# Issuing the fp32r products of K and of the expert layers in pieces of 256 columns instead of 512

## The reference

```
ln_c  : normalise over the 128 channels
q,k,v = w_qkv (768 x 128) applied to the channels; 8 heads of 32
k     = softmax of k over the 1024 pixels
ctx   = k v^T per head; out = ctx^T q;  x = x + w_out out + b_out

t     = x as tokens (16 x 1024 tokens of 128);  tn = ln_t(t)
w     = softmax(mean over images of tn @ Wr + br)      # 8 experts per pixel
for each expert e:
    h = relu(bn1(tn @ W1[e] + b1[e]))
    h = relu(bn2(h  @ W2[e] + b2[e]))
    y += w[:, e] * (h @ Wo[e] + bo[e])
x     = t + y
```

## Time and profile before

| what | us |
|---|---|
| median of 3 runs | 821.94 |
| lowest and highest | 819.64, 822.42 |
| the profiled execution, whole | 819.77 |
| its span, first to last instruction | 818.0 |
| PE busy in the span | 791.9 (97%), 4186 products |
| PEld busy | 669.9 (82%), 4186 loads |
| DVE, ACT, POOL busy | 525.6, 443.5, 578.8 |
| mean granted clock of TensorE | 0.989 of full |

### The profile page before, as it was taken

One profiled execution on the slowest core, in us unless ns is written; L12 is line 12 of the kernel. 1 busy time (PEld: TensorE's weight loads), 2 busy tenths in 40 slices (PEclk: granted clock), 3 DMA queues, 4 the chain that ended last, 5 costly groups with the idle time before them and its releaser, 6 DMA issues.

```text
span 818.0 us, 12728 instructions
## 1 busy us (share of the span) xinstructions
PE 791.9 (97%) x4186; PEld 669.9 (82%) x4186; DVE 525.6 (64%) x999; ACT 443.5 (54%) x560; POOL 578.8 (71%) x497
## 2 busy tenths in 40 slices
PE   6999999999998799999999999999999999999997
PEld 5998999999987678888888888888888888888885
DVE  4688777877865446665665656656656566565663
ACT  2576767767675554554554545545455455454542
POOL 5558788787857168667766776777777776677665
PEclk9999999999999889999999999999999999999999
DMA  7124344343342160210101201102022020110100
GB/s 240 53 79 161 123 163 147 112 170 128 131 154 103 54 231 1 78 65 13 77 26 51 77 0 77 54 23 77 1 77 77 0 77 26 51 77 0 51 26 26
DMA packets 22107, 64.52 MB, mean 79 GB/s; under 512 B 2608, under 2 KB 6840, under 8 KB 22080
## 3 DMA queue, kind: packets, MB, share of 16 engines
q1 hardware_dynamic: 22080, 64.19, 21.4%
HBM read 38.98 MB, written 25.20 MB: 78 GB/s over the span
## 4 chain that ended last, share of the span: by engine, by line
PE 64%; ACT 1%; DVE 0%; POOL 0%; POOLq 0%; issue 0%; DVEq 0%
PE psum L552 63%; PE psum L505 1%; PE psum L621 0%; POOL xn_lo L1045 0%; POOLq L83 0%; ACT h_hi L731 0%; PE psum L608 0%; DVE x_res L985 0%; DVE w_raw L928 0%; ACT xn_hi L743 0%; ACT route_all L767 0%; PE psum L584 0%; ACT feat_most L754 0%; ACT z_early L736 0%; ACT xn2T L695 0%
## 5 line engine op out<-in xcount | busy, mean ns | idle before, releaser
L912 DVE SCALAR_TENSOR_TENSOR h_lo<-psum,h_hi 128x1024 fp32r<-128x1024 f32 x128 | 156.8, 1225 | 207.4 <-ACT h_hi L731 207.4
L731 ACT ACTIVATE h_hi<-psum 128x1024 fp32r<-128x1024 f32 x128 | 131.3, 1026 | 255.9 <-PE psum L552 255.9
L1045 POOL TENSOR_TENSOR h_lo<-w_raw,h_hi 128x1024 fp32r<-128x1024 f32 x64 | 154.1, 2408 | 53.5 <-ACT h_hi L743 53.5
L552 PE MATMUL psum<-h_hi,w_hi 128*128 128x512 f32 x384 | 120.4, 395 | 1.7 <-DVE w_raw L928 0.9
L928 DVE SCALAR_TENSOR_TENSOR w_raw<-psum,minus_t,route_all 128x1024 f32<-128x1024 f32 x94 | 119.9, 1275 | 1.3 <-DMA route_all<-route_scratch 1.3
L552 PE MATMUL psum<-h_hi,w_lo 128*128 128x512 f32 x384 | 120.5, 395 | 0.0
L552 PE MATMUL psum<-h_lo,w_hi 128*128 128x512 f32 x384 | 119.5, 393 | 0.0
L1045 POOL TENSOR_TENSOR xn_lo<-w_raw,xn_hi 128x1024 fp32r<-128x1024 f32 x32 | 78.1, 2441 | 51.9 <-ACT xn_hi L743 51.9
L1045 POOL TENSOR_TENSOR xn_lo<-feat_most,xn_hi 128x1024 fp32r<-128x1024 f32 x32 | 77.2, 2413 | 51.0 <-ACT xn_hi L743 51.0
L1024 POOL TENSOR_TENSOR ln<-ln,const 128x8 f32<-128x8 f32 x32 | 52.6, 1643 | 57.6 <-DVE ln L896 57.6
L552 PEld LDWEIGHTS psum<-h_hi,w_hi 128*128 128x128 f32 x384 | 72.7, 190 | 17.5 <-issue 1.3
(11 more groups left out here) (146 smaller groups left out, 1445.1 us busy)
## 6 DMA issues: line engine op xcount, KB each, us to landing
route_all<-in_x SPq DMA_DIRECT2D x16, 512.0 KB, 3.9
x_res<-in_x SPq DMA_DIRECT2D x16, 512.0 KB, 3.3
x_scratch<-x_res SPq DMA_DIRECT2D x16, 512.0 KB, 2.8
xn_scratch<-xn SPq DMA_DIRECT2D x16, 512.0 KB, 2.6
xs_in<-xn_scratch SPq DMA_DIRECT2D x16, 512.0 KB, 4.5
x_res<-x_scratch SPq DMA_DIRECT2D x16, 512.0 KB, 3.2
out<-x_res SPq DMA_DIRECT2D x15, 512.0 KB, 2.6
route_all<-route_scratch SPq DMA_DIRECT2D x6, 512.0 KB, 6.2
```

The source lines that it names most:

```text
L552: mm = pe.matmul(dst[:, px], w[:, which, e, :], part[:, px], start=first and w is w_hi and part is hi, stop=last and part is lo, skip_grou ...
L731: nc.scalar.activation(h1_hi[r][:], z1[r], ACT.Relu).then_inc(h1_hi_done, 1)
L912: nc.vector.scalar_tensor_tensor(out=h1_lo[r][:], in0=z1[r], scalar=0.0, in1=h1_hi[r][:].bitcast(F32), op0=ALU.max, op1=ALU.subtract).then ...
L1045: nc.gpsimd.tensor_tensor(h2_lo[r][:], h2w[r], h2_hi[r][:].bitcast(F32), ALU.subtract).then_inc(h2_lo_done, 1)
```

## The change: pieces of 256 columns

A constant `PIECE = 256` is added. In `k_half` each product of 512 columns becomes two of 256 columns, one behind the other, with the same weights. In `layer` the loop over two banks becomes a loop over four pieces, again inside the loop over the three part products. The columns, the sums and the order of the part products stay. Only the first piece in a bank carries the start flag.

```
+PIECE = 256
@@ k_half
                     for w, xs in ((wkT_hi, xn_hi), (wkT_lo, xn_hi), (wkT_hi, xn_lo)):
-                        mm = pe.matmul(k_out[j][:, px], w[:, half], xs[p][:, px],
-                                       start=w is wkT_hi and xs is xn_hi, stop=xs is xn_lo)
+                        for m in range(BANK // PIECE):
+                            part = slice(px.start + PIECE * m, px.start + PIECE * (m + 1))
+                            mm = pe.matmul(k_out[j][:, part], w[:, half], xs[p][:, part],
+                                           start=w is wkT_hi and xs is xn_hi and m == 0, stop=xs is xn_lo, skip_group_check=True)
                     mm.then_inc(k_done, 1)
@@ layer
                 for w, part in ((w_hi, hi), (w_lo, hi), (w_hi, lo)):
-                    for n in range(2):
-                        px = slice(BANK * n, BANK * (n + 1))
+                    for n in range(PIXELS // PIECE):
+                        px = slice(PIECE * n, PIECE * (n + 1))
                         mm = pe.matmul(dst[:, px], w[:, which, e, :], part[:, px],
-                                       start=first and w is w_hi and part is hi, stop=last and part is lo, skip_group_check=True)
+                                       start=first and w is w_hi and part is hi and px.start % BANK == 0,
+                                       stop=last and part is lo, skip_group_check=True)
```

## The result

The change costs 12 us. The median of four runs is 832.91 us (832.47 to 833.89) against 820.79 (818.98 to 822.42, four runs), a ratio of 1.0157 with a 95% interval of 1.0135 to 1.0179. The direction and the wide range of the forecast (825, 805 to 864) held. Its size didn't: +3 was forecast, and the forecast's own range, 820 to 830, was missed too.

A forecast was written before the change was run, and what follows sets the result against it. PE was taken to bound the kernel; 2490 pairs at +1.2 ns add 3.0 us to the profiled 819.77, giving 822.8, and the median's 2.2 above the profiled run made it 825. Own range 820 to 830, wide range 805 to 864.

The forecast's parts named there:

- PE bounds both kernels, only the pitch counts: Whole kernel: its time is PE's time, so only two products of 256 columns against one of 512, start to start, matter.
- 2490 products more, each with its own load: K and the layers: 192 plus 2298 products are split, adding 2490 weight loads, from two to four per part product.
- Rival 4: Split products: the chip leaves out a repeated load of the same weights; no chance given.
- The load is hidden beneath 256 columns: Split products: a load occupies 0.111 to 0.114 us and just fits beneath a stream of at least 0.107 us.
- rival 3: Split products: loads don't hide beneath dense fp32r streams, so each piece pays load and stream; +553 us, about 1375, chance 0.05.
- The price of a pair, +1.2 ns: K and the layers: two pieces cost 1.2 ns more than one product of 512, the middle of two ends; +3.0 us.
- 15.7 ns: Products of 512 columns at full clock: the measured pitch of 229.0 ns beyond the 213.3 ns their columns need.
- lower end: Split pairs: the excess is a slower stream, 2.24 columns a ns, and halves with the columns; a pair costs 229.0, change nothing.
- upper end: Split pairs: a rate and a fixed 2.4 ns per product, as fp32 showed; 2490 x 2.4 = 6.0 us.
- Rival 1: Split products: the excess is a fixed start-up per fp32r product, a pair costs 244.7; +39.1 us, 861, chance 0.22.
- Rival 2: Split products: short streams run at full rate and the load limits, a pair costs 223; -15 us, 807, chance 0.20.
- K as 192 pairs of the same price: K's products: their pitch of 0.234 instead of 0.229 changes nothing, as they are only 192 pairs.

## Why the prediction was wrong

- **PE bounds both kernels, only the pitch counts.** Right. Nothing else on the page moved but one pause of 3 us, and the pitch gives 13.6 us, where 12.1 (medians) and 14.1 (profiles) were measured.
- **2490 products more, each with its own load.** Right, 6676 are listed. Rival 4 is out.
- **The load is hidden beneath 256 columns.** Right: 111.2 and 111.4 by itself in the fp32r streams of 128 and 192, as the fp32 rows had given. Load and stream one behind the other would have cost some 550 us (rival 3). The rule of the Trainium skill (TensorE: Matmul & The Clock Gate, "What overlaps and what doesn't"), that a load overlaps products only when its row group differs, is refuted for fp32r at this density by the 117.9 ns of a piece with its load.
- **The price of a pair, +1.2 ns.** This is the step that failed, in two ways. Its lower end, that the 15.7 ns are a slower stream and halve with the columns, is wrong: at a difference of 0 the excess is per product, 13.3 ns at 256 to 512 columns alike, and in the kernel's layers it is 16.5 at 512 and 11.2 at 256, where a rate would leave 8.2. (The 15.7 itself was 0.8 short, being read from window counts.) I had three signs for a rate, and none was one. The excess vanished at half clock, but a fixed excess does so as well. The last pair before a pause took 0.63 us as all others, but the end of a product is modelled in these records, and a duration can't show what a pitch does. And fp32's rows are silent on fp32r; they were also misread, for 0.109 us on 128 columns are two cycles at 2.4 GHz per column, not two half-clocked ones. The upper end, +2.4, took fp32's fixed part for fp32r's. Measured is 5.9 per pair of the layers, 2298 x 5.9 = 13.6 us, where the term had 2490 x 1.2 = 3.0; K, changed alone, cost nothing (819.54 against 819.33). Why a piece costs 117.9 here and not the 113.3 that the same tiles also showed stays open.
- **Rival 1, fixed 15.7 per product, +39 us.** Its mechanism is right at a difference of 0, where the change costs 30.4. It was 27 us off here because the price of a product isn't one number.
- **Rival 2, a piece at 111 to 112, -15 us.** For K's pieces it came near (113.3 in most rounds), and with strips at 192 for all of them, where the change gained 14.0. The reason given (a long stream that runs dry) isn't what was found.
- **K as 192 pairs of the same price.** Wrong, though it moved the time by about 1 us only, and to be seen in the earlier trace rows had I asked: 234 instead of 230 for the same product is a sign that place matters. I called it nothing because it was few pairs.
- **What would show it.** The marks were 873, 855, 817, 897 and 443 products in 100 us. 851 came (848 by the starts), next to "rate and the fixed part in full", which is close to the right number by luck, for a wrong reason; only the streams at several widths separated them.

## What to carry to other kernels

Where a pitch has a part that its columns don't explain, one width can't tell a rate from a fixed part: a stream of the same product at three widths can, in one short run, for the placement it has. If two places in one profile show different pitches for the same instruction, as 230 and 234 here, the reason may be worth more than the change at hand: three strips of 64 bytes gained 7.6 us, and the best width depended on the strips. A pitch may also have more than one stable value at one placement, so look at it before and behind each pause before you credit a change with it. For fp32r, compare placements at the width in use, and widths at a fixed placement, before either is called better.

## What the runs showed of the hardware

- fp32r products back to back at 2.4 GHz cost N/2.4 plus 13.3 ns from 256 to 512 columns, with the moving operand at the weights' address modulo 256 bytes. bf16 products in the same program pay 2.5.
- This excess goes with the difference of the two start addresses: in steps of 32 bytes 226.6 to 233.9 ns for 512 columns and 113.4 to 120.0 for 256, with a period of 256 bytes. A moving operand 4 bytes off had 240 and 123.
- At differences of 64 and 192 bytes the pitch of 256 columns has two stable values, 113.3 and 117.8, and can change from one to the other at a pause, either way.
- Loads of 128 fp32r weight columns hold the pitch at 111.2 and 111.4 ns when 128 and 192 columns move.
- Other engines at work on SBUF and PSUM changed the pitch by less than 0.1 ns (at 64); the order of banks and repeated weights changed it by nothing (at 0).
